# First batch: keys and links ahead of the second score step; output ahead of the gate; second router half and fourth split in other places

## What is computed

```python
x = x + L0_attn(layernorm(x))      # gated linear attention, 16 heads of 16
x = x + L0_xattn(ctx, layernorm(x))  # 0.6*sigmoid(ctx@Wi + ctx@Wj + b) + 0.4*layernorm(x)
x = x + L0_ffn(layernorm(x))       # 16 experts, top 6 by softmax, one shared expert
x = x + L1_attn(layernorm(x))      # softmax attention with rotary positions
x = x + L1_xattn(layernorm(x), ctx)
x = x + L1_ffn(layernorm(x))

# L0_attn, per head, per position t
q, k, v = silu(x@Wq), silu(x@Wk), silu(x@Wv)
S_t = exp(ld)*S_(t-1) + k_t v_t^T ;  o_t = q_t S_t
o = o * sigmoid((x@Wg1)@Wg2);  o = o * rsqrt(mean(o*o) + eps) * norm_w;  out = o@Wo

# ffn
probs = softmax(x@gate_w.T);  weights, chosen = top_k(probs, 6)
y = sum_e combine[:, e] * (silu(x@w1g_e.T) * (x@w1u_e.T)) @ w2_e.T  +  shared expert
```

## Time and profile before

| | |
|---|---|
| median of 3 runs | 925.93 us (925.31 to 926.55) |
| the profiled execution | 926.81 us |
| its span in the trace | 924.7 us |
| instructions | 14,203 |
| TensorE matmuls busy | 895.0 us, 97% |
| VectorE / ScalarE / GpSimd busy | 614.1 / 426.1 / 107.1 us |
| mean granted TensorE clock | 0.994 of full speed |
| read from HBM | 35.27 MB |

### The profile page before, as it was taken

One profiled execution on the slowest core, in us unless ns is written; L12 is line 12 of the kernel. 1 busy time (PEld: TensorE's weight loads), 2 busy tenths in 40 slices (PEclk: granted clock), 3 DMA queues, 4 the chain that ended last, 5 costly groups with the idle time before them and its releaser, 6 DMA issues.

```text
span 924.7 us, 14203 instructions
## 1 busy us (share of the span) xinstructions
PE 895.0 (97%) x5377; PEld 687.3 (74%) x5377; DVE 614.1 (66%) x1182; ACT 426.1 (46%) x1065; POOL 107.1 (12%) x131
## 2 busy tenths in 40 slices
PE   7997999999999999999999999999999999999998
PEld 4664778888888786667867777777766778888886
DVE  4568756666665757666787687777786566666665
ACT  7364634333433459883344343434344443333342
POOL 4003100000000130001233232323210000000000
PEclk9899999999999999999999999999999999999999
DMA  6004011111100230004500000000010111111001
GB/s 186 1 2 138 14 37 52 35 51 51 51 0 1 84 144 2 2 1 159 191 1 1 1 1 1 1 1 1 1 35 18 35 52 51 44 41 51 17 0 46
DMA packets 12537, 37.10 MB, mean 40 GB/s; under 512 B 2080, under 2 KB 4352, under 8 KB 11712
## 3 DMA queue, kind: packets, MB, share of 16 engines
q1 hardware_dynamic: 12448, 36.32, 11.9%
q0 software_dynamic: 32, 0.01, 0.0%
HBM read 35.27 MB, written 1.05 MB: 39 GB/s over the span
## 4 chain that ended last, share of the span: by engine, by line
PE 84%; DVE 7%; ACT 6%; issue 1%; DMA 1%; SPq 0%; POOL 0%; DVEq 0%; ACTq 0%
PE ps L1334 78%; PE ps L1962 3%; PE ps L1507 2%; ACT Q L1121 1%; DMA X<-in_x 1%; DVE stats L460 1%; DVE xn L468 1%; DVE P L536 1%; ACT whi L1136 0%; ACT silu_g L1161 0%; DVE weighted_h L684 0%; ACT probs_q L1236 0%; ACT h_hi L1166 0%; DVE h_lo L694 0%; DVE probs_q L853 0%
## 5 line engine op out<-in xcount | busy, mean ns | idle before, releaser
L1166 ACT ACTIVATE h_hi<-weighted_h 128x512 fp32r<-128x512 f32 x100 | 63.2, 632 | 154.2 <-DVE weighted_h L684 152.1
L694 DVE TENSOR_TENSOR h_lo<-weighted_h,h_hi 128x512 fp32r<-128x512 f32 x100 | 69.2, 692 | 66.5 <-ACT h_hi L1166 66.3
L1334 PE MATMUL ps<-xT_first,whi 128*128 128x512 f32 x376 | 111.3, 397 | 1.2 <-ACT silu_g L1161 1.2
L1334 PE MATMUL ps<-xT_second,whi 128*128 128x512 f32 x376 | 108.5, 391 | 1.3 <-ACT silu_g L1161 1.2
L720 DVE TENSOR_TENSOR shared_gate<-silu_g,row_shares 128x512 f32<-128x512 f32 x88 | 60.8, 691 | 63.5 <-ACT silu_g L1161 63.4
L1161 ACT ACTIVATE silu_g<-ps 128x512 f32<-128x512 f32 x100 | 59.7, 597 | 78.1 <-PE ps L1334 77.9
L1334 PE MATMUL ps<-xT,merged_q 128*128 128x256 f32 x384 | 91.9, 383 | 0.0
L1326 POOL TENSOR_TENSOR latent_rot<-rope_buf 128x256 f32<-128x256 f32 x96 | 68.5, 734 | 180.2 <-DVE rope_buf L808 180.2
L1334 PEld LDWEIGHTS ps<-xT_first,whi 128*128 128x128 f32 x376 | 70.3, 188 | 19.0 <-issue 2.8
L1334 PEld LDWEIGHTS ps<-xT_second,whi 128*128 128x128 f32 x376 | 70.1, 188 | 17.1 <-issue 2.5
L1334 PE MATMUL ps<-h_hi,wlo 128*128 128x512 f32 x200 | 78.4, 392 | 0.0
(11 more groups left out here) (197 smaller groups left out, 1569.0 us busy)
## 6 DMA issues: line engine op xcount, KB each, us to landing
raw<-in_ffn SPq DMA_DIRECT2D x50, 384.0 KB, 3.0
wx<-in_wx SPq DMA_DIRECT2D x4, 2048.0 KB, 11.1
cx<-in_cx SPq DMA_DIRECT2D x1, 1536.0 KB, 6.6
X<-in_x SPq DMA_DIRECT2D x4, 256.0 KB, 7.3
kvc<-in_kvc SPq DMA_DIRECT2D x1, 1024.0 KB, 14.3
out<-X SPq DMA_DIRECT2D x4, 256.0 KB, 2.2
wqkv<-in_wqkv SPq DMA_DIRECT2D x1, 768.0 KB, 8.5
wqkv<-in_wqkv SPq DMA_DIRECT2D x1, 512.0 KB, 6.8
```

Source lines behind the costliest of these rows:

```text
L694: v.tensor_tensor(h_lo[:, u % 2, :], weighted_h[:, u % 2, :], h_hi[:, u % 2, :].bitcast(F32), ALU.subtract).then_inc(act_lo[l], 1)
L1166: a.activation(h_hi[:, u % 2, :], weighted_h[:, u % 2, :], ACT.Copy).then_inc(act_hi[l], 1)
L1334: return pe.matmul(o, l, r, start=start, stop=stop, skip_group_check=True)
```

## The change

In layer 0's attention, for batch 0 alone, TensorE makes `keys(1)` and `links(0)` ahead of score step 1, `gate_inner(1)` and `links(1)` between score steps 1 and 2, and `values(1)` behind score step 2; ScalarE copies `gate_inner(1)` ahead of `links(0)`. In batches 2 and 3 `output0(a - 2)` stands ahead of `gate(a)`. In layer 0's experts, `logits_by_token(0, 1)` stands ahead of gate half 3 instead of behind it, VectorE's `router_maxima(0, 1)` ahead of `act_low` 2, the split of chunk 3 behind silu 3 (ScalarE) and behind `router_probabilities` (VectorE), and ScalarE loads the table of exponentials right behind `copy_logits(0, 1)`. Layer 1 keeps its order. No instruction is added and none taken away.

```diff
--- before.py
+++ after.py
@@ -700,11 +700,12 @@
 
             def experts(l):
                 weight_shared(l, 2)
+                if l == 0:
+                    router_maxima(l, 1)
                 act_low(l, 2, 2)
-                if l == 0:
-                    v.wait_ge(w_lo[0], EARLY)
-                split_lo(l, 3, 3)
-                router_maxima(l, 1)
+                if l == 1:
+                    split_lo(l, 3, 3)
+                    router_maxima(l, 1)
                 for i, last in blocks(v):
                     for u in range(2 * RING):
                         n = i * (2 * RING) + u
@@ -722,6 +723,9 @@
                             weight(l, n, u, shared_gate)
                         if isinstance(n, int) and n == EARLY:
                             router_probabilities(l, 1)
+                        if l == 0 and isinstance(n, int) and n == EARLY:
+                            v.wait_ge(w_lo[0], EARLY)
+                            split_lo(l, 3, 3)
                         act_low(l, n, u)
                         if isinstance(n, int) and n == EARLY:
                             router_choice(l, 1)
@@ -978,8 +982,6 @@
                             squares(b)
                         queries(c)
                         keys(c)
-                        if period == 0:
-                            links(0)
                         if period >= 1:
                             a.preload_act_table_set(LN_EXP)
                         if period >= 2:
@@ -987,6 +989,8 @@
                         if period >= 1:
                             root(b)
                         gate_inner(c)
+                        if period == 0:
+                            links(0)
                         values(c)
                         if period == 0:
                             links(1)
@@ -1011,6 +1015,7 @@
                 tokens_high(0, 1)
                 act_high(0, 1, 1)
                 copy_logits(0, 1)
+                a.preload_act_table_set(LN_EXP)
 
             def squares(b):
 
@@ -1168,7 +1173,8 @@
             def experts(l):
                 a.wait_ge(pe_down[l], 1)
                 act_high(l, 2, 2)
-                split_hi(l, 3, 3, 0)
+                if l == 1:
+                    split_hi(l, 3, 3, 0)
                 logit_exponentials(l, 1)
                 for i, last in blocks(a):
                     for u in range(2 * RING):
@@ -1557,32 +1565,35 @@
                         pe.wait_ge(g1_ready, 1)
                         pe.wait_ge(v_ready, 2)
                     scores_by_key(a, 0)
+                    if a >= 2:
+                        output0(a - 2)
                     if a >= 1:
                         gate(a)
-                    if a >= 2:
-                        output0(a - 2)
                     if a >= 1:
                         for quarter in range(4):
                             mixed_values(b, quarter)
                     if c < NB:
                         queries(c)
+                    if a == 0:
+                        keys(c)
+                        pe.wait_ge(xb_loaded, 16 * 2)
+                        links(0)
                     scores_by_key(a, 1)
-                    if c < NB:
+                    if a == 0:
+                        gate_inner(c)
+                        links(1)
+                    elif c < NB:
                         keys(c)
                     else:
                         mixed_values(a, 2)
                         mixed_values(a, 3)
-                    if a == 0:
-                        pe.wait_ge(xb_loaded, 16 * 2)
-                        links(0)
-                    else:
+                    if a >= 1:
                         sums_of_squares(b)
                     scores_by_key(a, 2)
+                    if 1 <= a < NB - 1:
+                        gate_inner(c)
                     if c < NB:
-                        gate_inner(c)
                         values(c)
-                    if a == 0:
-                        links(1)
                     if c + 1 < NB:
                         pe.wait_ge(g1_ready, c + 1)
                         transposed_tokens(0, c + 1)
@@ -1800,8 +1811,10 @@
                         elif last and u == 2 * RING - 2:
                             pass
                         elif u < 2 * RING - 1:
+                            if l == 0 and isinstance(n, int) and n == EARLY - 1:
+                                logits_by_token(l, 1)
                             gate_half(l, n + 1, i, last, u + 1)
-                            if isinstance(n, int) and n == EARLY - 1:
+                            if l == 1 and isinstance(n, int) and n == EARLY - 1:
                                 logits_by_token(l, 1)
                             up_half(l, n + 1, i, last, u + 1)
                         elif not last:
```

## The result

| | before | after |
|---|---|---|
| median, same chip | 926.24 us (924.83 to 927.16, 6 runs) | 921.01 us (920.27 to 922.74, 6 runs) |
| ratio to before, 95% interval | | 0.9949 [0.9935, 0.9962] |
| the profiled execution, its span | 926.81 us, 924.7 us | 920.27 us, 918.1 us |
| TensorE matmuls busy | 895.0 us | 891.0 us |
| mean granted TensorE clock | 0.994 | 0.998 |

The kernel is faster, by 4.7 us by the ratio (926.24 x 0.0051). The prediction said 7.3 us, to 918.6, and a range of 917.2 to 921.2. Taken from its own 925.93 us the ratio puts the kernel after at 921.2 (925.93 x 0.9949), the slow edge of the range. Over two us of the sum didn't come. Two executions, one of the kernel before (beside e5 to e8) and one of e7, took 5,033.9 and 5,051.3 us for a reason that nothing here shows; they are counted as slow, and no ratio uses them.

What follows compares the result with a forecast made beforehand. TensorE was taken as the bound, 84% of the chain, with gains only where it stands or runs slowly. 5.10 + 0.83 + 1.39 = 7.32 us off 926.81 gives 919.5, lowered 0.88 to 918.6; range 917.2 to 921.2 us.

Steps and rivals of the forecast that it cites:

- First batch, 5.10 us: First batch: keys and links fill TensorE's 3.49 us gap, clock stays 1.00, next batch's scores at 30.57 against 35.67 us.
- Output ahead of gate, 0.83 us: Last batch: the output product runs while ScalarE's copies finish, so TensorE's 0.83 us wait with `gate` goes.
- It is hidden: Last batch: ScalarE's 0.4 us wait for first expert weights delays nothing; split ends at 76.7, `root` wanted at 77.25.
- rival (c): First weights come late on ScalarE, delaying `root`; the output swap gives nothing, 919.4 us; chance 0.06.
- It is passed on if VectorE follows: Last batch: the 0.83 us gain counts if VectorE follows; its next product had waited 1.14 us for TensorE.
- Second router half, 1.39 us: Start of the experts: earlier exponentials let silu 3 end at 113.57, not 115.81 us; TensorE's whole 1.39 us wait goes.
- Rival (d): Start of the experts: table load costs twice its row, 2.56 us; third part gives 0.2 us, 919.8 us; chance 0.04.
- The prediction's sum by that page: Start of the experts, 2.66 us per table switch: silu 3 at about 115.7 us, third part's gain some 0.2 us.
- Rival (b), the second low stretch moves: Low clock near 87 us shifts: 920.1 us if earlier or longer, 917.6 if it misses the sum-of-squares product; chance 0.13.
- rival (a): First batch: the clock falls all the same, gain 2.5 in place of 5.10 us, 921.2 us; chance 0.12.

Runs made afterwards that it cites:

- e5: Changed kernel with GpSimd's three splits each moved to where VectorE has only PSUM-operand work or statistics: 916.41 us, ratio 0.9902.
- e8: Kernel before with only the output product moved ahead of the gate: 927.55 us, ratio 1.0011.
- e7: Kernel before, own order, with 13 matmuls of zeros filling TensorE's 3.5 us gap in the first batch: 924.28 us, ratio 0.9983.
- e9: Kernel before with only the third part, second router half earlier and fourth split later: 924.28 us, ratio 0.998.
- e1: Changed kernel with the gate again ahead of the output product in batches 2 and 3: 920.97 us, ratio 0.9943.
- e6: Changed kernel with GpSimd's three splits spread and the gate back ahead of the output product: 917.04 us, ratio 0.9905.
- e2: Changed kernel with GpSimd's three splits waiting until VectorE has made batch 2's `on`: 920.39 us, ratio 0.9938.
- e3: Changed kernel with GpSimd's three splits waiting only for the four normalises: 920.27 us, ratio 0.9927.
- e10: Changed kernel with GpSimd's splits spread, plus three constant products in TensorE's late waits: 914.94 us, ratio 0.9871.
- e11: Changed kernel with GpSimd's splits spread, repeated on one chip beside the version with three constant products: 915.62 us, ratio 0.9876.

## Why the prediction was wrong, step by step

- **First batch, 5.10 us.** The mechanism was right to the instruction: clock 1.00, the two short gaps (0.71 and 0.16 us), F of 7.34 for 7.22. The size failed: it was that of one profile. Against e8 and e9 the same change saves 3.95 us, and the part alone measured 3.3. With it goes a slip in the sum: the prediction took 7.32 us off the profiled 926.81 and then lowered the result by the 0.88 us that profile stood above the median, though a long low stretch, which the change removes, may be what put it there. Without that shift the same sum says 919.5.
- **Output ahead of gate, 0.83 us.** This step failed. By the landmarks of the two profiles the whole miss lies here (7.32 us were summed and 5.37 came, and this part is 2.01 off, its +1.18 against -0.83); by the times of the parts alone it is +1.0 us for -0.83, as far off as the first part's 3.3 for 5.10. In the third batch the swap cost nothing, as said: from batch 1's first scores to the last batch's 31.46 us pass before (67.13 - 35.67) and 31.42 after (61.19 - 29.77). The gate's wait did go, ScalarE's wait for weights came as said (0.46 us for 0.4), and "It is hidden" held: against the first scores `root` comes 10.95 us before (78.08 - 67.13) and 10.07 after (71.26 - 61.19). So rival (c) did not come. What failed is "It is passed on if VectorE follows": VectorE was asked only for its next product, not for the normalises behind it. The trace of before had the sign, unread: four normalises at 1.81 us and an `on` pair at 2.42 beside GpSimd, where the earlier batches' pairs take 0.73 and 0.88. The swap brings VectorE's normalises and ScalarE's second split 0.88 us earlier against the first scores (11.18 to 10.30, 12.21 to 11.32), but the first split of GpSimd, tied to the landing of the weights, by 0.31 only (10.06 to 9.75). So the normalises lie half a us deeper under split one, their last falls under split two, and it waits for all of it: 1.90 us for 0.41. The prediction's bounds for this step, 0 to 0.83, and its rivals left no room for a loss in it. Undone (e1), alone (e8) and freed of the splits (e5 against e6, where the swap gives 0.88) this holds in the landmarks of every profile. In the times it is less clear: e1 and the changed kernel can't be told apart, nor can e5 and e6, and e8 rules out the gain but not a swap that costs nothing. That the splits cost time is clear: spread, they take the ratio from 0.9949 to 0.9902, with intervals that do not meet.
- **Second router half, 1.39 us.** Right: 1.57 in the profiles, 1.85 [0.5, 3.3] alone. Rival (d), a table load that costs more than its row, did not come: silu 3 follows the load by 0.01 us (108.11 - 106.82 - 1.28) in the kernel after. The Trainium skill's drain of some 1380 ns (ScalarE: Activation LUTs, What ACT_TABLE_LOAD costs) is not seen in this trace. The prediction's sum by that page is a little off: silu 3 would end at 115.8 us, not 115.7, which leaves no gain where it says 0.2; nothing else hangs on it.
- **Rival (b), the second low stretch moves**, had the place and nearly the price: T is 8.9 us without it and 9.9 to 12.0 with it, by what it falls on. The clock reads 0.50 for some 3.4 us in the profiles of before and after, and for longer in e1 (83.7 to 90.4 us), e2 (82.0 to 88.7) and e3 (80.5 to 90.7). In these three profiles it hides most or all of what S had won: `og` comes 18.80, 18.34 and 18.03 us after the first scores (19.98 in the changed kernel), T takes 11.10, 10.68 and 12.00, and the router's product comes 29.90, 29.02 and 30.03 us after them (29.85 in the changed kernel). That the like times of e1, e2 and e3 come from this is likely and not shown, since only one execution of each has a trace. It does not explain the miss of the two profiles, since T is 9.87 after and 9.88 before.

The parts alone measured -3.3, +1.0 and -1.85 us, together -4.15; the change measured -4.7 [-3.5, -6.0]. That agrees.

That the result lies at the edge of the range and not beyond it is luck: the range reached to 921.2 us for rival (a), a clock that falls all the same, and that did not happen. Not tried: whether the first low stretch's two lengths can be steered.

## What to carry to other kernels

When a step brings an engine forward, list everything that engine runs in the next few us and what its neighbours do at that moment; an operation that is slower at one place than at the same line elsewhere (0.41 us and 1.90) is a collision that a shift can make worse. Read a gain that hangs on the clock from several profiles, not from one. And try harmless products in short waits of TensorE: with three of them the clock stayed at 1.00 in four runs of four and T fell from 10.61 to 8.93 us. In the time it is 0.7 us by the medians of e10 and e11, four runs each, which their intervals do not tell from nothing; the runs lay closer together (0.7 us from end to end, 1.3 without them).

## What the runs showed of the hardware

**GpSimd's splits lock VectorE out.** Tiles view of the kernel after, the durations (smallest, middle, largest in ns) of VectorE's `xn` and `on` between 70 and 78 us, of one shape each:

```profile
L468 DVE TENSOR_SCALAR xn<-X,mv,rstd x4: 403/907/1904, 71.5 to 73.5; 128x256 f32<-128x256 f32 x4
```

```profile
L506 DVE SCALAR_TENSOR_TENSOR on<-og,normw,rrec x2: 472/1244/2017, 75.3 to 77.2; 128x256 f32<-128x256 f32 x2
```

A blocked one takes what is left of the split, up to its whole 1.81 us and some more; it is not slowed in proportion. Whether VectorE holds up GpSimd in the same way is not clear from these traces: the second and third split together took 3.90 us before and 3.61 after. VectorE operations with a PSUM operand are untouched: the product `P<-ps,DT` at 76.04 us before takes 2.36 us as ever, with a split from 77.19 on, and so are the batch statistics in e10 (0.75 us at 77.60, under a split at 77.76). The Trainium skill, SBUF — State Buffer, 🔬 SBUF: two separate sides, says it: the pair of ports that the two engines share "is an **exclusive lock**, not a bandwidth split", taken by a VectorE operation with two SBUF inputs or in a two-port mode. The traces agree for the products of two SBUF inputs, and they show the float32 TENSOR_SCALAR blocked as well; whether it runs in a two-port mode no trace tells.

**One gap, two lengths of low clock.** The same 3.49 us gap was followed by about 6.9 us at the 1.2 GHz level in two profiles and about 3.4 in two others, and a later one began at some 68.7 us in e9, and again at 89.2 there, where the other profiles that have one begin it between 80.5 and 87.3. Its length differs too: about 3.4 us in e5 and e11, 6.8 in e1 and e2, 10.2 in e3. The profile of e6 has none with the waits still there; with the first gap closed and the late waits filled (e10) the mean clock read 1.00 in four runs of four.
